# Graph attention on one core: gathers with a row limit, so that edges outside a visit's block are not fetched

## The chip, the cores and the metric

The kernel runs on one core of a Trainium2 chip. The metric is the device time of one execution in microseconds (us); the time before is the median of three runs. Nothing else runs on the core.

## The reference, cut to what matters

Three graph attention layers over 3125 nodes and 50000 edges, then a mixture-of-experts step. Only the attention layer matters here; the edges are sorted by their target `dst`.

```python
z = (x @ W).reshape(N, num_heads, head_dim)          # 12 x 64, 12 x 64, 1 x 768
el = jnp.sum(z * attn_l, axis=-1)
er = jnp.sum(z * attn_r, axis=-1)
e = jax.nn.leaky_relu(el[src] + er[dst], NEG_SLOPE)
m = jax.ops.segment_max(e, dst, num_segments=N)
ex = jnp.exp(e - m[dst])
denom = jax.ops.segment_sum(ex, dst, num_segments=N)
msg = (ex / denom[dst])[:, :, None] * z[src]
out = jax.ops.segment_sum(msg, dst, num_segments=N) + z + bias
```

## The kernel before

Nodes stand in 25 blocks of 128 (`NB`, padded to `NPAD` = 3200 rows). Each of the three layers has two parts. The node sweep multiplies every block by the weights and writes rows of `z` with the heads' `el` behind them to a table in device memory (`table[l]`, 792 floats used per row in layers 0 and 1, 769 in layer 2). The edge sweep then goes over the edges.

Edges stand in 391 tiles of 128 (50048 places, 48 of them padding). A tile whose edges belong to two blocks of targets is visited twice, once for each block: 391 + 24 = 415 visits (`V`), in 83 groups of 5 (`G`). The table `src_k` holds for each visit the 128 source rows, `dst_k` the target's place inside the visit's block. A place outside 0 to 127 gives a one-hot column of zeros in `S`, so such an edge adds nothing to the sum.

For each visit GpSimd issues one indirect DMA (L672) that gathers 128 table rows into one of 20 row buffers (`U` = 20: 15 in `arena`, 5 in `W`). It waits until the visit 20 places earlier has been summed (`s_agg`). Completion is counted on that buffer's own semaphore `s_z`. VectorE waits for all five gathers of a group (L1475 in layers 0 and 1, L1457 in layer 2), forms the exponents from them (L1475 and L1480), ScalarE takes the exponential, VectorE multiplies each row by its weight (L1492; the result stands in the row buffer itself), and TensorE adds the visit up with the one-hot `S` (L1047), which frees the buffer. Where a visit's place among the 20 is in `SPLIT`, ScalarE and VectorE split the row in two parts (L781, L1509; L785, L1512 and L1513 in layer 2), so that TensorE can take the faster number format. VectorE also makes the transposed one-hot from byte codes once a group (L1445). In layer 2 the one head's weight goes into the one-hot (`S_weighted`, L1498), and VectorE has less to do.

GpSimd's queue is written out for all 1245 gathers; each one is queued behind the one before it. VectorE's order within a group is fixed by `weigh`: message 0, message 1, then the steps of the next group's exponents between messages 1 to 3.

`tables` (L1279 to L1286 of the kernel before) makes `src_k` and `dst_k` once, before the first node sweep. TensorE's first node sweep and GpSimd's first gathers wait for it (`s_tables`).

Of the kernel before, what the change touches and what calls it, by code (L numbers as in the profile page):

```python
# [8 lines left out]
I32 = mybir.dt.int32  # L9
U32 = mybir.dt.uint32  # L10
U8 = mybir.dt.uint8
ALU = mybir.AluOpType
# [3 lines left out]
P = 128  # L16
# [3 lines left out]
NPAD = NB * P  # L20
# [8 lines left out]
ER_LEAD = 3  # L29
U = G * NBUF  # L30
VISITS = ET + NB - 1
V = -(-VISITS // G) * G
NG = V // G
# [14 lines left out]
NS = (TOP * N + EX * (P - 1)) // P  # L48
# [8 lines left out]
class Chain:  # L57
# [5 lines left out]
    def link(self, instruction):  # L63

        self.mark(instruction)
        self.follow()
# [33 lines left out]
def gnn_ffn(nc, x, edges, gnn, ffn, out):  # L100
    with ExitStack() as ctx:
        def sb(name, shape, dt=F32):
            return ctx.enter_context(nc.sbuf_tensor(name, shape, dt))

        def sem(name):
            return ctx.enter_context(nc.semaphore(name))
# [9 lines left out]
        PS = ctx.enter_context(nc.psum_tensor("PS", [P, 8, 512], F32))  # L116
# [19 lines left out]
        with nc.sbuf_tensor("xT_rest", [P, 2, D], F32R) as xT_rest:  # L136
            with nc.sbuf_tensor("local_rows", [P, 4 * P], BF16) as local_rows:
                below = EX * 2 * 2 * HALF - KC * (D + 2 * HMAX) - 2 * D - 2 * P
# [27 lines left out]
        src_k = sb("src_k", [P, V], I32)  # L166
        dst_k = sb("dst_k", [P, V])
        b_k = sb("b_k", [1, V + 1], I32)
        b_g = sb("b_g", [1, NG, 4], I32)
        b_of = sb("b_of", [1, NG + ER_LEAD, 8], I32)  # L170
        ends = sb("ends", [1, NB], I32)
        turns = sb("turns", [1, NS], I32)
        erm = sb("erm", [P, NB, 2 * HMAX])
        ert = sb("ert", [P, NB, HMAX])
        erp = sb("erp", [P, NB * 3 * 2 * HMAX], BF16)
# [19 lines left out]
        wu = sb("wu", [P, G, 2 * HMAX])  # L195
# [9 lines left out]
        def rows_buf(j, q, width=D):  # L205
            return arena[:, (2 * j + q) * D:(2 * j + q) * D + width]
# [4 lines left out]
        in0, in1, in2, xr, xT, x2 = (lambda q, j=j: rows_buf(j, q) for j in range(6))  # L211
# [22 lines left out]
        s_z = [sem(f"s_z{j}") for j in range(U)]  # L234
# [22 lines left out]
        def sweep_nodes(eng, stages, chain=None, per=0, count=NB, rolled=True, start=0):  # L257


            def steps(i, ts):  # L260
                for t in ts:
                    for stage, lead in stages:
                        if i is not None or 0 <= t + lead < count:
                            stage(Block(t + lead, i))

            if not rolled:
                steps(None, range(-max(lead for _, lead in stages), count - min(lead for _, lead in stages)))
                return
            steps(None, range(start - max(lead for _, lead in stages), 2))
            trips = (count - 4) // 2  # L270
            with eng.Fori(1, 1 + trips) as i:
                if chain:
                    chain.enter(i - 1, per)
                steps(i, (0, 1))
            if chain:
                chain.leave(trips)
            steps(None, range(2 + 2 * trips, count - min(lead for _, lead in stages)))
# [24 lines left out]
        def table_width(l):  # L302
            return D + (2 * HEADS[l] if HEADS[l] > 1 else 1)

        def slot_width(l):

            return D + 2 * HEADS[l]
# [10 lines left out]
        def edge_row(l, at):  # L318
            return group_rows(l, at // G)[:, at % G, :]

        def edge_heads(l, jj, n=1):
            return group_rows(l, jj)[:, :, D:D + n * HEADS[l]]
# [4 lines left out]
        def er_of(l, jj):  # L327
            return group_bank(jj)[:, 0:G * 2 * HEADS[l]].rearrange("p (g h) -> p g h", g=G)
# [11 lines left out]
        def uses(jj):  # L340

            return NI if jj < LAST_GROUPS else NI - 1

        def prep(at, n):
            return ST[:, :, :, :].rearrange("p a b c -> p (a b c)")[:, at:at + n]
# [4 lines left out]
        def bk_f():  # L350
            return prep(V, V)
# [4 lines left out]
        def rows_f():  # L356
            return prep(3 * V, 4 * 2 * P)
# [224 lines left out]
        def _(pool):  # L582
# [70 lines left out]
            for l in range(3):  # L653
                if l == 1:
                    pool.wait_ge(s_base, 16 * NB)
                    pool.wait_ge(s_spare, 16)
                    pool.wait_ge(s_last_bias, 16)
                if l == 2:
                    pool.wait_ge(s_bias_added, 16 * NB)
                sweep_nodes(pool, [(store(l), 0)])  # L660
                pool.wait_ge(s_stored[0], 16 * (NB // 2 + 1) * (l + 1))
                pool.wait_ge(s_stored[1], 16 * (NB // 2) * (l + 1))
                pool.wait_ge(s_tab, NB * (l + 1))
                pool.wait_ge(s_tables, 1)
                pool.wait_ge(s_filled, 16 * 2 * 3)
                pool.sem_inc(s_tick)
                for k in range(V):
                    pool.wait_ge(s_agg, V * l + k + 1)
                    if l == 2 and k == 12 * D // slot_width(l):
                        for q in range(2):  # L670
                            pool.wait_ge(s_x_kept[q], 16 * (NB // 2 + 1 - q))
                    nc.gpsimd.indirect_dma_start(  # L672
                        edge_row(l, k % U)[:, 0:table_width(l)], None, table[l][:, :],
                        bass.IndirectOffsetOnAxis(src_k[:, k:k + 1].bitcast(U32), 0)).then_inc(s_z[k % U], 16)

            for b in range(NB):
                keep_rows(b)
# [521 lines left out]
        def _(dve):  # L1199
            dc = Chain(dve, s_dve)  # L1200
            link = dc.link
# [10 lines left out]
            def augment_first(ks):  # L1212
                for k in ks:
                    for j in range(2):
# [14 lines left out]
            below = rows_f()[:, 0:(NB - 1) * 4].rearrange("p (b c) -> p b c", c=4)  # L1229
# [9 lines left out]
                                                op0=ALU.add, op1=ALU.add))  # L1239
            link(nc.vector.scalar_tensor_tensor(out=enter_at, in0=own[0:NB - 1, :], scalar=1.0, in1=PS[0:NB - 1, 1, 4:5],  # L1240
                                                op0=ALU.add, op1=ALU.add))
# [10 lines left out]
                                                op0=ALU.mult, op1=ALU.add))  # L1252
# [25 lines left out]

            def tables():  # L1279
                dve.wait_ge(s_turned, 1)  # L1280
                link(nc.vector.tensor_copy(src_k[:, :], PS[:, 2, 0:V]))
                link(nc.vector.scalar_tensor_tensor(out=dst_k[:, :], in0=bk_f(), scalar=-float(P), in1=PS[:, 3, 0:V],
                                                    op0=ALU.mult, op1=ALU.add))
                if V > VISITS:
                    link(nc.vector.memset(dst_k[:, VISITS:V], NO_NODE))
                dve.sem_inc(s_tables, 1)  # L1286

            W_parts = [(l, k, j) for l in (1, 2) for k in range(KC) for j in range(2)]
# [150 lines left out]
            def edge_sweep(l):  # L1439
                H = HEADS[l]  # L1440
# [7 lines left out]
                def exponents(g, i, jj):  # L1448

                    er = er_of(l, jj)  # L1450
                    t, u = wt[:, jj, :, 0:H], wu[:, :, 0:H]

                    def logits():
                        dve.wait_ge(s_er, g + (NG * l + 1))
                        for j in range(jj * G, (jj + 1) * G):
                            dve.wait_ge(s_z[j], 16 * i + 16 * (uses(jj) * l + 1))
                        dc.mark(nc.vector.tensor_tensor(u, edge_heads(l, jj), er[:, :, 0:H], ALU.add))  # L1457

                    def leaky():
                        dc.follow()  # L1460
                        dc.mark(nc.vector.scalar_tensor_tensor(out=u, in0=u, scalar=SLOPE, in1=u, op0=ALU.mult, op1=ALU.max))

                    def less_bound():
                        dc.follow()
                        dc.mark(nc.vector.tensor_tensor(u, u, er[:, :, H:2 * H], ALU.subtract))

                    def limit():
                        dc.follow()
                        nc.vector.tensor_scalar(t, u, 0.0, None, ALU.min).then_inc(s_pre, 1)

                    def both_logits():
                        dve.wait_ge(s_er, g + (NG * l + 1))
                        for j in range(jj * G, (jj + 1) * G):
                            dve.wait_ge(s_z[j], 16 * i + 16 * (uses(jj) * l + 1))
                        dc.mark(nc.vector.scalar_tensor_tensor(out=wu[:, :, 0:2 * H], in0=edge_heads(l, jj, 2), scalar=shift[:, 0:1],  # L1475
                                                               in1=er, op0=ALU.subtract, op1=ALU.add))

                    def higher():
                        dc.follow()
                        nc.vector.tensor_tensor(t, u, wu[:, :, H:2 * H], ALU.max).then_inc(s_pre, 1)  # L1480

                    if H > 1:
                        return both_logits, higher
                    return logits, leaky, less_bound, limit
# [235 lines left out]
            t = routing("t")[:, 0:EX * EX].rearrange("p (e f) -> p e f", f=EX)  # L1720
# [3 lines left out]
            t = routing("t").rearrange("p (m e) -> p m e", e=EX)  # L1724
# [135 lines left out]
```

## Time and profile before

| | us |
|---|---|
| runs | 2811.25, 2812.51, 2815.1 (median 2812.51) |
| span of the profiled execution | 3059.8 |

The profile has no other time of its own for that execution; its span runs from the first to the last instruction and is the time that the rows below are read against. It is 247.3 us longer than the median of the runs. Set-up and the first node sweep end at about 246 us, the three edge sweeps lie at about 246 to 906, 1095 to 1760 and 1960 to 2610 us, with a node sweep ahead of each, and the experts' part fills the last 300 us.

### The profile page before, as it was taken

To read this page: it belongs to the slowest core of one execution; us is meant where nothing else is said; L and a number is where in the kernel's file an instruction comes from. 1 tells how busy PE (TensorE), PEld (TensorE's weight loads), DVE (VectorE), ACT (ScalarE), POOL (GpSimd) and SP (SyncE) were. 2 spreads that over 40 slices of the span, in tenths; PEclk is the share of its full clock that TensorE was granted. 3 is DMA by queue.
4 is the path that set the end of the run, shared out by engine and by line. 5 is a ranking of instruction groups with operands and counts; after the bars stand their busy time and mean duration, and the time that the engine had idled before them with its cause. 6 is when DMAs were issued, how large, how long until landed. Compare 5 with 4: busy or idle time off the path is not lost.

```text
span 3059.8 us, 57119 instructions
## 1 busy us (share of the span) xinstructions
PE 2691.3 (88%) x14056; PEld 1838.6 (60%) x14060; DVE 2096.8 (69%) x3895; ACT 1244.9 (41%) x2607; POOL 1506.0 (49%) x1528
## 2 busy tenths in 40 slices
PE   3997999998989979898989999788898889759998
PEld 2884555555558855555555578555555555547776
DVE  6776888888887768888878877545555555673332
ACT  1224555555544435555555544223222223622211
POOL 1005666666631156666666412466666665114443
PEclk9998999999999979999999999899999999979999
DMA  6447888888867878888888767788888887967776
GB/s 210 169 148 251 289 286 291 291 290 290 289 219 205 210 228 292 289 287 290 291 287 288 250 191 216 218 281 285 279 282 281 282 282 258 397 217 145 145 146 118
DMA packets 199261, 762.09 MB, mean 249 GB/s; under 512 B 41889, under 2 KB 58033, under 8 KB 198542
## 3 DMA queue, kind: packets, MB, share of 16 engines
q0 software_dynamic: 127632, 604.14, 64.8%
q1 hardware_dynamic: 53790, 108.21, 11.6%
q10 hardware_dynamic: 17760, 48.79, 4.0%
q8 instruction: 36, 0.59, 0.1%
q14 instruction: 43, 0.35, 0.0%
HBM read 640.01 MB, written 133.45 MB: 253 GB/s over the span
## 4 chain that ended last, share of the span: by engine, by line
PE 50%; DVE 21%; issue 13%; ACT 4%; DMA 4%; another core or an unknown queue 3%; SPq 2%; POOL 1%; DVEq 1%; ACTq 1%; POOLq 0%
PE PS L1047 30%; DVE arena L1492 5%; PE PS L1176 5%; PE PS L978 4%; PE PS L1165 4%; PE PS L980 2%; DVE parts L1509 2%; PE PS L1022 2%; DMA arena<-table,src_k 2%; SPq L493 1%; DVE ST_b L1445 1%; DVE arena L1357 1%; DVE arena L1367 1%; DVE arena L1335 1%
## 5 line engine op out<-in xcount | busy, mean ns | idle before, releaser
L672 POOL DMA_INDIRECT arena<-table,src_k x945 | 959.9, 1016 | 500.8 <-issue 213.1
L1047 PE MATMUL PS<-arena,S 128*128 128x384 f32 (+1 forms) x1848 | 706.8, 514 | 57.8 <-issue 46.3
L1492 DVE TENSOR_TENSOR arena<-arena,PS 128x768 f32<-128x768 f32 x630 | 575.2, 946 | 0.9 <-ACT arena L822 0.9
L1047 PEld LDWEIGHTS PS<-arena,S 128*128 128x128 f32 x1848 | 335.5, 194 | 282.7 <-issue 156.8
L1047 PE MATMUL PS<-parts,S 128*128 128x384 f32 (+2 forms) x1332 | 340.4, 375 | 57.2 <-issue 51.0
L672 POOL DMA_INDIRECT W<-table,src_k x300 | 295.9, 986 | 160.5 <-PE PS L1047 71.2
L1047 PE MATMUL PS<-arena,S_weighted 128*128 128x384 f32 (+1 forms) x840 | 319.9, 516 | 33.4 <-issue 25.3
L1022 PEld LDWEIGHTS PS<-erp,ST_b 128*128 128x128 bf16 x3735 | 193.9, 97 | 249.9 <-issue 184.2
L618 POOL DMA_DIRECT2D table<-arena x75 | 41.6, 555 | 557.7 <-DVEq L1379 382.3
L1047 PEld LDWEIGHTS PS<-parts,S 128*128 128x128 f32 x1332 | 223.7, 192 | 106.0 <-issue 97.5
L830 ACT ACTIVATE apart<-iota_row,dst_k 128x128 f32<-128x128 f32 x830 | 261.7, 389 | 60.8 <-issue 44.1
L781 ACT ACTIVATE parts<-arena 128x780 fp32r<-128x780 f32 x168 | 142.0, 849 | 309.2 <-DVE arena L1492 136.7
L1022 PE MATMUL PS<-erp,ST_b 128*128 x3735 | 213.0, 172 | 54.0 <-issue 38.9
L1047 PE MATMUL PS<-W,S 128*128 128x396 f32 (+1 forms) x640 | 239.8, 502 | 14.6 <-issue 8.1
L1047 PEld LDWEIGHTS PS<-arena,S_weighted 128*128 128x128 f32 x840 | 154.3, 196 | 143.7 <-issue 79.4
L978 PE MATMUL PS<-W_lead,S 128*128 128x512 f32 x450 | 190.4, 423 | 9.8 <-DVE xT_rest L1383 7.9
L1509 DVE TENSOR_TENSOR parts<-arena,parts 128x780 fp32r<-128x780 f32 x168 | 162.0, 964 | 35.7 <-issue 24.4
L1492 DVE TENSOR_TENSOR W<-W,PS 128x768 f32<-128x768 f32 x200 | 182.4, 944 | 0.0
L978 PE MATMUL PS<-W_lead,xT_rest 128*128 128x512 f32 x450 | 179.2, 398 | 0.0
L978 PE MATMUL PS<-W_rest_r,S 128*128 128x512 f32 x450 | 178.7, 397 | 0.0
L1047 PEld LDWEIGHTS PS<-W,S 128*128 128x128 f32 x640 | 116.1, 190 | 91.3 <-issue 39.0
L1795 DVE TENSOR_SCALAR arena<-PS,gate_of 128x768 f32<-128x768 f32 x56 | 57.0, 1018 | 162.5 <-PE PS L1176 162.5
(293 smaller groups left out, 4354.1 us busy)
## 6 DMA issues: line engine op xcount, KB each, us to landing
arena<-mixed SPq DMA_DIRECT2D x63, 384.0 KB, 3.6
table<-arena POOLq DMA_DIRECT2D x50, 396.0 KB, 3.3
local_b<-local SPq DMA_DIRECT2D x123, 160.0 KB
mixed<-sums ACTq DMA_DIRECT2D x50, 384.0 KB
arena<-table SPq DMA_DIRECT2D x50, 384.0 KB, 4.6
arena<-table,src_k POOLq DMA_INDIRECT x945
table<-arena POOLq DMA_DIRECT2D x25, 384.5 KB, 4.6
out<-last_bias POOLq DMA_DIRECT2D x25, 384.0 KB, 6.4
```

The costliest lines, as they stand in the source:

```text
L672: nc.gpsimd.indirect_dma_start(edge_row(l, k % U)[:, 0:table_width(l)], None, table[l][:, :], bass.IndirectOffsetOnAxis(src_k[:, k:k + 1]. ...
L781: nc.scalar.activation(parts[:, n, 0, 0:D + H], row[:, 0:D + H], ACT.Copy).then_inc(s_leading, 1)
L830: o = nc.scalar.activation(apart[:, j, :], iota_row[:, :], ACT.Abs, scale=-1.0, bias=dst_k[:, bass.ds(g * G + j, 1)])
L978: nc.tensor.matmul(PS[:, 4 + 2 * b.q, :], rows[x_part], W_parts[W_part][:, 0:512], start=start, stop=stop)
L980: o = nc.tensor.matmul(PS[:, 5 + 2 * b.q, 0:z_width(l) - 512], rows[x_part], W_parts[W_part][:, 512:z_width(l)], start=start, stop=stop)
L1022: o = nc.tensor.matmul(er_of(l, jj)[:, j, :], ST_b[:, jj, j * P:(j + 1) * P], erp[:, bass.ds(b * (6 * H) + part * 2 * H, 2 * H)], start=(p ...
L1047: o = nc.tensor.matmul(flat[:, bass.ds(odd * 1024 + 512 * c, n)], onehot, row[:, c * HALF:c * HALF + n], start=False, stop=True, skip_grou ...
L1165: o = nc.tensor.matmul(to, token_xT(b.q)[:, k * P:(k + 1) * P], WiT[:, k, bass.ds(e * FF, FF)], start=(k == 0), stop=(k == KC - 1))
L1176: o = nc.tensor.matmul(PS[:, 4 + 2 * b.q + c, 0:HALF], hT(b.q)[0:rows, j * P:(j + 1) * P], flat[0:rows, bass.ds(e * (2 * D) + (2 * c + j) ...
L1492: nc.vector.tensor_tensor(z, z, a, ALU.mult).then_inc(s_msg, 1)
L1509: nc.vector.tensor_tensor(low[:, 0:D + H], row[:, 0:D + H], f32(high[:, 0:D + H]), ALU.subtract).then_inc(s_rest, 1)
L1795: nc.vector.tensor_scalar(zr(b.q, D).rearrange("p (c d) -> p c d", c=2), PS[:, 4 + 2 * b.q:6 + 2 * b.q, 0:HALF], gate_of[:, bass.ds(b.n, 1 ...
```

## The change

It passes a limit to the indirect DMA (`bounds_check`), under which a row whose source index lies past `NPAD` - 1 is not fetched and raises no error. `tables` adds `NPAD` or more to the source of every edge whose place lies outside the visit's block, for visits from the 21st on (`U:`). The first 20 visits fetch all rows, so that every row buffer holds finite numbers. What a skipped row's buffer holds afterwards is that of an earlier visit, so the exponents of layers 0 and 1 are held at or below zero (`higher`). Three small tables become bytes instead of 32-bit integers (`b_g`, `b_of`, `turns`). The limit is handed over in a register of GpSimd's queue, which is written again ahead of each gather; the wait for `s_agg` then stands on that register instruction instead of the gather.

```diff
@@ -166,10 +166,10 @@
-        b_g = sb("b_g", [1, NG, 4], I32)
-        b_of = sb("b_of", [1, NG + ER_LEAD, 8], I32)
+        b_g = sb("b_g", [1, NG, 4], U8)
+        b_of = sb("b_of", [1, NG + ER_LEAD, 8], U8)
         ends = sb("ends", [1, NB], I32)
-        turns = sb("turns", [1, NS], I32)
+        turns = sb("turns", [1, NS], U8)
@@ -671,7 +671,8 @@
                     nc.gpsimd.indirect_dma_start(
                         edge_row(l, k % U)[:, 0:table_width(l)], None, table[l][:, :],
-                        bass.IndirectOffsetOnAxis(src_k[:, k:k + 1].bitcast(U32), 0)).then_inc(s_z[k % U], 16)
+                        bass.IndirectOffsetOnAxis(src_k[:, k:k + 1].bitcast(U32), 0),
+                        bounds_check=NPAD - 1, oob_is_err=False).then_inc(s_z[k % U], 16)
@@ -1278,11 +1279,16 @@
                 dve.wait_ge(s_turned, 1)
-                link(nc.vector.tensor_copy(src_k[:, :], PS[:, 2, 0:V]))
                 link(nc.vector.scalar_tensor_tensor(out=dst_k[:, :], in0=bk_f(), scalar=-float(P), in1=PS[:, 3, 0:V],
                                                     op0=ALU.mult, op1=ALU.add))
                 if V > VISITS:
                     link(nc.vector.memset(dst_k[:, VISITS:V], NO_NODE))
+                link(nc.vector.tensor_copy(src_k[:, 0:U], PS[:, 2, 0:U]))
+                below, beyond = prep(2 * V, V - U), prep(3 * V, V - U)
+                link(nc.vector.tensor_scalar(below, dst_k[:, U:], 0.0, float(NPAD), ALU.is_lt, ALU.mult))
+                link(nc.vector.tensor_scalar(beyond, dst_k[:, U:], float(P), float(NPAD), ALU.is_ge, ALU.mult))
+                link(nc.vector.tensor_tensor(below, below, beyond, ALU.add))
+                link(nc.vector.tensor_tensor(src_k[:, U:], below, PS[:, 2, U:V], ALU.add))
                 dve.sem_inc(s_tables, 1)
@@ -1477,7 +1483,8 @@
                     def higher():
                         dc.follow()
-                        nc.vector.tensor_tensor(t, u, wu[:, :, H:2 * H], ALU.max).then_inc(s_pre, 1)
+                        nc.vector.scalar_tensor_tensor(out=t, in0=u, scalar=0.0, in1=wu[:, :, H:2 * H],
+                                                       op0=ALU.min, op1=ALU.max).then_inc(s_pre, 1)
```

On VectorE, at the end of the set-up before the first node sweep, the kernel before has these rows (the table of sources first, then that of places):

```order
L1342 TENSOR_TENSOR W_rest_r<-W,W_lead 128x792 x6
L1281 CAST src_k<-PS 128x415
L1282 SCALAR_TENSOR_TENSOR dst_k<-ST,PS 128x415
L1402 MEMSET gm 128x12
L1310 BN_STATS stats<-arena 128x6
```

The changed kernel has at the same place:

```order
L1348 TENSOR_TENSOR W_rest_r<-W,W_lead 128x792 x6
L1282 SCALAR_TENSOR_TENSOR dst_k<-ST,PS 128x415
L1286 CAST src_k<-PS 128x20
L1288 TENSOR_SCALAR ST<-dst_k 128x395
L1289 TENSOR_SCALAR ST<-dst_k 128x395
L1290 TENSOR_TENSOR ST<-ST 128x395
L1291 TENSOR_TENSOR src_k<-ST,PS 128x395
L1408 MEMSET gm 128x12
L1316 BN_STATS stats<-arena 128x6
```

Four instructions are added, each over 395 columns, and one shrinks from 415 columns to 20; nothing else of VectorE's order moves there.

On VectorE, within a group of an edge sweep of layers 0 and 1, the kernel before has:

```order
L1445 TENSOR_SCALAR ST_b<-local_b,own_code 128x640
L1475 SCALAR_TENSOR_TENSOR wu<-arena,shift,PS 128x120
L1492 TENSOR_TENSOR arena<-arena,PS 128x768
L1480 TENSOR_TENSOR wt<-wu 128x60
L1492 TENSOR_TENSOR arena<-arena,PS 128x768 x2
```

The changed kernel has:

```order
L1451 TENSOR_SCALAR ST_b<-local_b,own_code 128x640
L1481 SCALAR_TENSOR_TENSOR wu<-arena,shift,PS 128x120
L1499 TENSOR_TENSOR arena<-arena,PS 128x768
L1486 SCALAR_TENSOR_TENSOR wt<-wu 128x60
L1499 TENSOR_TENSOR arena<-arena,PS 128x768 x2
```

No row moves: one instruction of a group changes its kind. TensorE's, ScalarE's and SyncE's rows are the same in both kernels.

## Rows read from the trace of the kernel before

**Rows 1.** Busy time in stretches: 57 to 237 node sweep, 400 to 800 edge sweep, and so on.
```profile
core 0: us, PE busy (x) PEld busy (x) DVE busy (x) ACT busy (x) POOL busy (x), PEclk, DMA share, GB/s
57.00:237.00 180.00, 178.04 (x1030) 157.79 (x1031) 127.37 (x265) 44.70 (x73) 13.10 (x24) 1.00 0.47 162
400.00:800.00 400.00, 361.66 (x1801) 215.85 (x1800) 331.39 (x479) 221.00 (x526) 264.00 (x261) 0.98 0.88 289
906.00:1087.00 181.00, 176.10 (x989) 151.42 (x989) 136.56 (x214) 78.96 (x96) 31.50 (x44) 0.98 0.76 199
1200.00:1600.00 400.00, 359.82 (x1823) 215.20 (x1823) 334.48 (x482) 218.16 (x519) 263.90 (x260) 0.99 0.88 289
2100.00:2500.00 400.00, 356.80 (x1825) 216.90 (x1824) 216.16 (x677) 114.00 (x251) 255.87 (x261) 0.99 0.87 282
2747.00:3044.00 297.00, 296.29 (x1537) 232.40 (x1534) 93.41 (x166) 57.68 (x109) 136.18 (x105) 1.00 0.72 139
```

**Rows 2.** What VectorE waited for, 400 to 800 us: us in total, times, longest.
```profile
DVE wu L1475 <- remote: 43.4, 28, 4.2
DVE parts L1509 <- ACT parts L781: 9.2, 3, 4.7
DVE wu L1475 <- DMA W<-table,src_k: 6.0, 3, 2.3
DVE wu L1475 <- DMA arena<-table,src_k: 5.1, 4, 1.7
```

**Rows 3.** The same, 2100 to 2500 us (layer 2).
```profile
DVE wu L1457 <- remote: 103.3, 40, 6.5
DVE parts L1512 <- ACT parts L785: 45.0, 9, 7.7
```

**Rows 4.** GpSimd's gathers by line, whole execution: durations min/median/max, and what ended its idle time.
```profile
L672 POOL DMA_INDIRECT arena<-table,src_k x945: 941/950/1745, 246.3 to 2588.6; - x189
L672 POOL DMA_INDIRECT W<-table,src_k x300: 941/950/1727, 267.7 to 2566.0; - x150
  issue: 279.7, 906
  PE PS L1047: 277.3, 265
```

**Rows 5.** GpSimd in order of time, layer 1: start, us, what, idle before.
```profile
1300.76 1.04 POOL L672 DMA_INDIRECT arena<-table,src_k  x1 [1.15 <-PE PS L1047]
1302.11 0.94 POOL L672 DMA_INDIRECT arena<-table,src_k  x1 [0.30 <-issue]
1303.35 0.95 POOL L672 DMA_INDIRECT arena<-table,src_k  x1 [0.30 <-issue]
...
1308.45 0.94 POOL L672 DMA_INDIRECT arena<-table,src_k  x1 [1.30 <-PE PS L1047]
```

**Rows 6.** GpSimd's groups by line, 400 to 800 us: count, busy, mean ns, idle before.
```profile
L672 POOL DMA_INDIRECT arena<-table,src_k x196 | 201.8, 1030 | 101.7 <-PE PS L1047 46.4 <-issue 42.0 <-remote 13.3
L672 POOL DMA_INDIRECT W<-table,src_k x65 | 64.6, 994 | 34.6 <-issue 15.5 <-PE PS L1047 14.5 <-remote 4.6
```

**Rows 7.** The same, 2100 to 2500 us (layer 2).
```profile
L672 POOL DMA_INDIRECT arena<-table,src_k x195 | 191.7, 983 | 109.2 <-issue 42.4 <-PE PS L1047 41.4 <-remote 25.4
```

**Rows 8.** The page's GpSimd group of plain table stores, 128 rows each.
```profile
L618 POOL DMA_DIRECT2D table<-arena x75 | 41.6, 555 | 557.7 <-DVEq L1379 382.3
```

**Rows 9.** VectorE's exponent instructions by line: durations min/median/max.
```profile
L1480 DVE TENSOR_TENSOR wt<-wu x166: 205/214/272, 259.2 to 1746.0; 128x60 f32<-128x60 f32 x166
L1475 DVE SCALAR_TENSOR_TENSOR wu<-arena,shift,PS x126: 319/338/341, 258.9 to 1744.9; 128x120 f32<-128x120 f32 x126
L1461 DVE SCALAR_TENSOR_TENSOR wu<-wu x83: 154/161/200, 1965.8 to 2595.0; 128x5 f32<-128x5 f32 x83
L1457 DVE TENSOR_TENSOR wu<-arena,PS x63: 144/165/168, 1965.6 to 2593.6; 128x5 f32<-128x5 f32 x63
```

**Rows 10.** VectorE in order of time around `tables`.
```profile
51.16 0.58 DVE L1281 CAST src_k<-PS 128x415 int32<-128x415 f32 x1
51.78 0.59 DVE L1282 SCALAR_TENSOR_TENSOR dst_k<-ST,PS 128x415 f32<-128x415 f32 x1
52.55 0.07 DVE L1402 MEMSET gm<- 128x12 f32 x1 [0.18 <-DVE dst_k L1282]
54.24 0.56 DVE L1310 BATCH_NORM_STATS2 stats<-arena 128x6 f32<-128x384 f32 x1 [1.63 <-DMA arena<-in_x]
```

**Rows 11.** The page's DMA queues: packets, MB, share of 16 engines.
```profile
q0 software_dynamic: 127632, 604.14, 64.8%
```

## Prediction

> **What bounds the kernel now.** I read the busy time by stretch first, to see which parts can move at all. In the node sweeps and in the experts' part TensorE is busy 99%, 97% and nearly 100% of the time at a granted clock of 0.98 or more [rows 1]. The change touches nothing there. The edge sweeps are different. They take 400 us for 261, 260 and 261 gathers [rows 1], that is 1.533, 1.538 and 1.533 us a visit, although layer 2 gives VectorE only 216 us of work in 400 where layers 0 and 1 give it 331 and 334. A pace that does not depend on VectorE's load points to something common: the gathers. The DMA engines are busy 0.87 to 0.88 of the time at 282 to 289 GB/s.
>
> Next I read what VectorE waits for. In layer 0 it waits for gathers at L1475 (the rows that end in "remote" and "DMA") 43.4 + 6.0 + 5.1 = 54.5 us in 400, or 0.209 us a visit [rows 2]. Little else holds it, so its own pace without that wait would be 1.533 - 0.209 = 1.324 us. In layer 2 it waits 103.3 us for gathers [rows 3], but VectorE has slack there.
>
> Last comes GpSimd. Of 1245 gathers, 906 had only the fixed gap of about 0.30 us ahead of them [rows 4]; the timeline shows bursts of them, then one wait of more than 1 us for TensorE to free a buffer [rows 5]. Its own pace in layer 0 is (201.8 + 64.6)/261 + 0.30 = 1.321 us [rows 6], in layer 2 about 0.983 + 0.30 = 1.283 us [rows 7]. So VectorE and GpSimd are within 0.01 us of each other in layers 0 and 1, and both wait in the profiled execution on landings.
>
> **The profiled execution and the timed one.** The span is 3059.8 us, the median 2812.51. TensorE's stretches at 97% and more leave hardly any of the 247.3 us, so I put it on the 1245 visits: 0.199 us each. The timed visit then takes about 1.538 - 0.199 = 1.339 us. That is a choice, and the most important one here: it says that in a timed run most of the waiting for gathers (0.209 us a visit in layer 0) is already absent.
>
> **The change, part by part.**
>
> *Rows left out.* 415 visits ask for 53120 rows; 50000 are edges of their block, so 3120 are not. A block has about 2000 edges, 16 visits, so the first 20 visits contain one boundary, whose 128 rows are still fetched: 2992 rows a sweep are skipped, 5.6%, in all 8976. If every visit were set by the gathers' transfer, the profiled execution would gain 0.056 x 1.538 = 0.087 us a visit, 108 us over 1245. At the timed pace that is 0.056 x 1.339 = 0.075 us, 94 us, but the visit can't become shorter than the next bound. In layers 0 and 1 that is VectorE's 1.324: (1.339 - 1.324) x 830 = 12 us. In layer 2 it is GpSimd's 1.283: 0.056 x 415 = 23 us. Together 35 us at most. The other end is 0: if the landings no longer end any wait in the timed run. I take 25, since five gathers must land together and a queue seldom empties fully.
>
> *The register and the check on GpSimd.* No row shows a gather with a limit, nor a register write ahead of one. Below, the extra cost is 0: the check may be in the loop already, and the register write may lie under the gather before it. Less than nothing is possible for the two gathers at each boundary, which have half the descriptors to write; 72 boundaries by half of 0.95 us twice would be 68 us of GpSimd's time, most of which is not on the path. Above, the nearest rows are the indirect gather at 950 ns [rows 4] against the plain store of 128 rows at 555 ns [rows 8]: looking up 128 addresses costs at most 395 ns, 3.1 ns a row. A compare for each row should not cost more than half of that, 0.2 us. As GpSimd's pace in layers 0 and 1 (1.321) is only 0.018 below the timed visit, nearly all of an extra cost enters. For my forecast I take 0 to 0.02 us, so nothing; the larger values are a rival below. Behind a gather that waits stand all later gathers, and behind these VectorE's L1475.
>
> *tables.* Four instructions over 395 columns; the rows with 415 columns took 0.58 and 0.59 us [rows 10], so 4 x 0.57 = 2.3 us, less about 0.45 for the cast that shrinks to 20 columns: 1.8 us. Behind them VectorE sat idle 1.63 us for the first block of `x`, so 0.2 us shows. If that load came earlier, it would be 1.8. I take 0.2.
>
> *higher.* The old instruction takes 214 ns for 60 columns [rows 9]. The same two kinds over 5 columns take 161 and 165 ns, so the kind costs nothing: 0 us. The bound is the 338 ns of the same kind over 120 columns: 0.124 x 166 = 21 us; nearest is the 5-column pair, so I take 1 us.
>
> *Byte tables.* They are smaller and are read by as many instructions. 0 us.
>
> Sum against the span: 3059.8 - 108 + 1 is about 2955 if transfers bind there throughout; I expect about two thirds, near 2990. Sum against the median: 2812.5 - 25 + 0.2 + 1 = 2788.7, so 2789 us.
>
> **A rule beside it.** In this trace the gathers' landings end VectorE's waits at 289 GB/s [rows 1, 2]. The Trainium skill (DMA: Bandwidth & Descriptors, Anatomy of one DMA) gives a DMA of this kind about 2.0 us plus its bytes by 436 GB/s. By that a gather of 405.5 KB moves in 0.93 us, an estimate from that page, well inside every visit, and leaving rows out would gain nothing; the sum would be 2813.7. The rows of the profiled execution disagree, those of a timed run can't say.
>
> **Rivals.**
>
> *A: transfers still bind a little, GpSimd's extra is small.* 2789 us, range 2766 to 2806 (below: half of the 94 us, if the timed run waits for gathers more than the 1.339 us says; above: a quarter of the 25). For it: half of the groups wait for gathers in the profile. Chance 0.42.
>
> *B: the transfer is hidden anyway.* The whole 0.209 us is an effect of the profiled execution; VectorE and GpSimd at 1.32 set the timed pace. Then a shorter queue changes nothing: 2812.5 + 1.2, so 2808 to 2818. For it: 1.339 is that close to 1.324. Against it: layer 2, where VectorE is idle 46% of the time and the pace is no better. This holds too the case that a skipped row takes as long in the queue as a fetched one. Chance 0.18.
>
> *C: the check makes GpSimd the bound.* Place: the emission of L672. With x us more for each gather its pace is 1.321 + x in layers 0 and 1 and 1.283 + x in layer 2. It decides from 0.018 in the former and 0.056 in the latter. At x = 0.1: 0.082 x 830 + 0.044 x 415 = 86 us, 2898 us. At 0.05: 27 us, 2839 us. At 0.2: 211 us, 3023 us. For it: one instruction more for each gather, the wait moved off the gather, a compare for each of 128 rows, and no slack. Against it: all that the lookup costs is 3.1 ns a row, and the register write can lie under the gather before it. In the profiled execution, whose visit takes 1.538, this would not show as a loss up to 0.2 us. Chance 0.40.
>
> **How the numbers follow.** The likeliest is A, by little: 2789. The range leaves out the upper part of C, 0.13 (above x = 0.1), and 0.05 below 2766: 2766 to 2900. A difference under 0.2% (5.6 us) can't be told from no change. Faster 0.42, same 0.18, slower 0.40.
>
> **What would show it.** Right: fewer packets in the software queue by about 4500 of 127632 [rows 11] and 28 MB less; a shorter wait at VectorE's L1475 (now at another line); a profiled span well below 3059.8; GpSimd's gathers still at 0.95 us with a gap of 0.30. C shows as a longer gather or gap and a larger share of gathers with nothing but the gap ahead. B shows as a shorter span with unchanged runs and unchanged gathers. The weakest step is the 1.339 us: if the timed run waits for gathers more than I think, the gain is up to 94 us.

## The result and the profile after

The changed kernel is slower: 3023.69 us against 2811.88 us, a ratio of 1.0744 (95% interval 1.0722 to 1.0765). That is 212 us more. 2789 us was forecast, and the time lies outside the range of 2766 to 2900. One of its four runs (3743.59 us, at a mean granted clock of 0.654 where the others had 0.973 to 0.976) is a slow one and left out of the ratio. The profiled execution has a span of 3018.0 us and took 3019.67 us itself, so here the span and the runs agree.

Busy time in the same stretches of the edge sweeps, layers 0, 1 and 2 (columns as in [rows 1]):

```profile
400.00:800.00 400.00, 361.17 (x1850) 208.21 (x1851) 337.08 (x491) 224.07 (x537) 276.29 (x263) 1.00 0.86 278
1200.00:1600.00 400.00, 359.14 (x1837) 206.56 (x1836) 330.14 (x481) 218.93 (x524) 274.02 (x262) 1.00 0.85 276
2100.00:2500.00 400.00, 360.42 (x1862) 210.95 (x1861) 222.23 (x699) 118.34 (x261) 290.71 (x267) 1.00 0.85 274
```

The pace is 1.521, 1.527 and 1.498 us a visit. Beside [rows 1] this looks like a small gain (1.533, 1.538, 1.533). The runs say the opposite, because the profiled execution of before was 247 us slower than its own runs. No wait read from that trace may be compared with this one as it stands; further down stands what that trace has in common with a batch in which the kernel before took 3066 us.

What VectorE waited for, 400 to 800 us, and then 2100 to 2500 us:

```profile
DVE parts L1516 <- ACT parts L782: 24.1, 12, 5.0
DVE wu L1481 <- DMA arena<-table,src_k: 17.7, 15, 2.9
DVE wu L1481 <- PE PS L1023: 17.0, 17, 2.6
DVE wu L1481 <- DMA W<-table,src_k: 7.0, 4, 2.5
...
DVE wu L1463 <- DMA arena<-table,src_k: 46.1, 14, 5.3
DVE wu L1463 <- PE PS L1023: 44.7, 21, 3.2
```

L1481 is the old L1475, L1463 the old L1457, L1023 the old L1022. Against [rows 2] and [rows 3] the rows that end in "remote" are gone and a new releaser has come: `PE PS L1023`, the products of `er` with the one-hot (`er_of_edges`), which in these stretches of the trace of before released none. TensorE is late. But it is busy only 361 us in 400, so it is held up by something that isn't a matmul.

The page's queue row and its row of gathers, then two rows of TensorE's queue (`PEldq` in the profile), `blocks_of` (L1013) and the register operations of `add_up` (L1040), with durations min/median/max:

```profile
q0 software_dynamic: 127632, 576.01, 63.2%
L672 POOL DMA_INDIRECT arena<-table,src_k x945 | 1014.4, 1073 | 408.8 <-issue 226.3
L1013 PEldq TENSOR_LOAD <-b_of x498: 1216/1222/2532, 252.0 to 2552.9; - x166
L1040 PEldq ALU_OP  x640: 32/32/32, 266.4 to 2544.5; - x160
```

Three things are to be seen. The bytes fell by 28.1 MB from [rows 11], as forecast, but the packets did not: 127632 in both, so no packet falls away. 4458 more packets than before are under 512 bytes (46347 against 41889 in the pages), about one for two of the 8976 rows. A gather is longer: mean 1073 ns. And TensorE's queue spends 1222 ns, 498 times (twice a group), on reading five block numbers into registers from the table `b_of`. Not one row of the prediction was about this load. In the kernel before, with words in place of bytes, the same two rows of TensorE's queue read:

```profile
L1012 PEldq TENSOR_LOAD <-b_of x498: 5/582/1751, 249.9 to 2596.9; - x166
L1039 PEldq ALU_OP  x640: 2/32/755, 262.3 to 2588.9; - x160
```

The added instructions of `tables` in the changed kernel, in order of time (start, us, what, idle before):

```profile
51.11 0.18 DVE L1286 CAST src_k<-PS 128x20 int32<-128x20 f32 x1
51.32 0.37 DVE L1288 TENSOR_SCALAR ST<-dst_k 128x395 f32<-128x395 f32 x1
51.72 0.36 DVE L1289 TENSOR_SCALAR ST<-dst_k 128x395 f32<-128x395 f32 x1
52.12 0.57 DVE L1290 TENSOR_TENSOR ST<-ST 128x395 f32<-128x395 f32 x1
52.73 0.57 DVE L1291 TENSOR_TENSOR src_k<-ST,PS 128x395 int32<-128x395 f32 x1
53.48 0.07 DVE L1408 MEMSET gm<- 128x12 f32 x1 [0.18 <-DVE src_k L1291]
55.39 0.56 DVE L1316 BATCH_NORM_STATS2 stats<-arena 128x6 f32<-128x384 f32 x1 [1.85 <-DMA arena<-in_x]
...
L1486 DVE SCALAR_TENSOR_TENSOR wt<-wu x166: 204/213/278, 262.8 to 1723.1; 128x60 f32<-128x60 f32 x166
```

The last row is the new `higher`: 213 ns against 214 [rows 9]. Behind the added four VectorE still sits idle 1.85 us for the first block of `x`, so most of them is hidden. The first BATCH_NORM_STATS2 starts at 55.60 us in x2 and at 55.19 in x1 (two kernels of the second batch below, with and without the added four), so about 0.4 us shows. `higher` costs nothing.

### The profile page after: what moved, and what is told of

Same layout as the page of the kernel before. It is cut to its first block, busy times and chain, and to the rows that moved or that the text cites. A ratio compares the mean times of both kernels' runs of the same rounds, so it can differ in the third digit from the quotient of the medians.

```text
span 3018.0 us, 58368 instructions
## 1 busy us (share of the span) xinstructions
PE 2665.2 (88%) x14056; PEld 1784.5 (59%) x14060; DVE 2084.3 (69%) x3899; ACT 1241.7 (41%) x2607; POOL 1584.4 (52%) x1528
## 2 busy tenths in 40 slices
DMA packets 199271, 734.04 MB, mean 243 GB/s; under 512 B 46347, under 2 KB 62491, under 8 KB 198542
## 3 DMA queue, kind: packets, MB, share of 16 engines
q0 software_dynamic: 127632, 576.01, 63.2%
## 4 chain that ended last, share of the span: by engine, by line
PE 53%; DVE 15%; issue 12%; DMA 9%; ACT 4%; POOL 3%; SPq 2%; ACTq 1%; DVEq 1%; POOLq 0%
PE PS L1048 32%; DMA arena<-table,src_k 6%; PE PS L1177 5%; PE PS L979 4%; PE PS L1166 4%; PE PS L981 2%; DVE arena L1499 2%; POOL arena L672 2%; PE PS L1023 2%; DMA W<-table,src_k 2%; SPq L493 2%; DVE W L1499 1%; DVE arena L1341 1%; DVE arena L1363 1%; DVE arena L1362 1%
## 5 line engine op out<-in xcount | busy, mean ns | idle before, releaser
L672 POOL DMA_INDIRECT arena<-table,src_k x945 | 1014.4, 1073 | 408.8 <-issue 226.3
L1048 PEld LDWEIGHTS PS<-arena,S 128*128 128x128 f32 x1848 | 326.4, 191 | 338.5 <-issue 212.8
L672 POOL DMA_INDIRECT W<-table,src_k x300 | 318.6, 1062 | 121.8 <-issue 74.4
L1048 PE MATMUL PS<-parts,S 128*128 128x384 f32 (+2 forms) x1332 | 323.9, 365 | 25.4 <-issue 12.0
L1048 PE MATMUL PS<-arena,S_weighted 128*128 128x384 f32 (+1 forms) x840 | 313.8, 504 | 34.1 <-issue 20.1
L1023 PEld LDWEIGHTS PS<-erp,ST_b 128*128 128x128 bf16 x3735 | 173.8, 96 | 200.0 <-issue 135.2
L1048 PE MATMUL PS<-W,S 128*128 128x396 f32 (+1 forms) x640 | 247.0, 508 | 20.8 <-DVE arena L1499 13.1
L1048 PEld LDWEIGHTS PS<-arena,S_weighted 128*128 128x128 f32 x840 | 148.0, 190 | 148.9 <-issue 81.1
L1023 PE MATMUL PS<-erp,ST_b 128*128 x3735 | 182.1, 171 | 23.8 <-DVE ST_b L1451 16.2
L650 POOL DMA_INDIRECT out<-arena,target_of x56 | 89.1, 1591 | 159.1 <-DMA out<-arena,target_of 128.8
```

Of the source, the lines that this page charges most:

```text
L650: nc.gpsimd.indirect_dma_start(out[:, :], bass.IndirectOffsetOnAxis(target_of[:, n:n + 1].bitcast(U32), 0), zr(n % 2, D), None, compute_op ...
L672: nc.gpsimd.indirect_dma_start(edge_row(l, k % U)[:, 0:table_width(l)], None, table[l][:, :], bass.IndirectOffsetOnAxis(src_k[:, k:k + 1]. ...
L1023: o = nc.tensor.matmul(er_of(l, jj)[:, j, :], ST_b[:, jj, j * P:(j + 1) * P], erp[:, bass.ds(b * (6 * H) + part * 2 * H, 2 * H)], start=(p ...
L1048: o = nc.tensor.matmul(flat[:, bass.ds(odd * 1024 + 512 * c, n)], onehot, row[:, c * HALF:c * HALF + n], start=False, stop=True, skip_grou ...
```

## The experiments

Two theories went in: one of the parts that GpSimd executes (limit, register, wait apart) costs some 0.17 us a visit; or the byte tables cost it, on TensorE's queue. The kernels of one batch were run together with the kernel before; ratios are to it, and its median there is given.

### First: one part of the change at a time (before: 2811.93 us)

**e1, the byte tables alone.**

```diff
-        b_g = sb("b_g", [1, NG, 4], I32)
-        b_of = sb("b_of", [1, NG + ER_LEAD, 8], I32)
+        b_g = sb("b_g", [1, NG, 4], U8)
+        b_of = sb("b_of", [1, NG + ER_LEAD, 8], U8)
...
-        turns = sb("turns", [1, NS], I32)
+        turns = sb("turns", [1, NS], U8)
```

> The kernel before with the three small tables as bytes, and nothing else of the change. Theory W (the wait that moved from the gather to the register write ahead of it takes the slack away) and theory L (the limit itself makes each gather longer) both say no change: ratio 1.00. Theory B (byte tables make the register loads of TensorE or ScalarE slower) says up to the whole 212 us, ratio 1.07.

**e2, the byte tables and the limit**, no row left out (the lines of e1 and this one):

```diff
+                        bounds_check=NPAD - 1, oob_is_err=False).then_inc(s_z[k % U], 16)
```

> The kernel before with byte tables and the limit on every gather, but with the table of sources as before, so that no row lies past the limit and none is left out. Theories W and L say that the loss is all here or more of it, since no row is saved: ratio 1.07 to 1.09. Theory S (rows that are left out cost GpSimd or the queue more than rows that are fetched) says ratio 1.00.

**e3, the whole change, with the limit in a register that is written once**:

```diff
+            limit_reg = nc.alloc_register(mybir.EngineType.Pool, "row_limit")
+            nc.gpsimd.reg_mov(limit_reg, NPAD - 1)
+            limit = nc.gpsimd.snap(limit_reg)
...
-                        bounds_check=NPAD - 1, oob_is_err=False)
+                        bounds_check=limit, oob_is_err=False)
```

> The changed kernel, but the limit is put in a register once, ahead of all gathers, so each gather carries its own wait again and no register write stands before it. Theory W says the loss is gone and the skipped rows may gain a little: ratio 0.99 to 1.00, span near 2800 us. Theories L and S say it stays: ratio 1.07.

**e4, e1 with an instruction ahead of each gather that carries the wait**:

```diff
+                    pool.sem_inc(s_tick)
                     nc.gpsimd.indirect_dma_start(
```

> The kernel before with byte tables and no limit, but ahead of each gather stands a small instruction of GpSimd's queue that carries the wait (it adds 1 to a semaphore that nobody waits for). Theory W says ratio 1.07 as in the changed kernel. Theories L, S and B say 1.00.

Measured: e1 3022.57 us (1.0752 [1.0734, 1.077]), e2 3024.86 (1.0757 [1.0739, 1.0775]), e3 3019.21 (1.0737 [1.0719, 1.0755]), e4 3021.75 (1.0747 [1.0729, 1.0765]). The byte tables alone are the whole loss, and nothing that is added to them or taken from the rest moves it. In e1 TensorE's load takes 1222 ns again, and VectorE waits for TensorE (2100 to 2500 us):

```profile
L1012 PEldq TENSOR_LOAD <-b_of x498: 1216/1222/2597, 251.7 to 2554.7; - x166
...
DVE wu L1457 <- PE PS L1022: 80.1, 35, 3.0
```

The theory of the bytes stands, that of GpSimd's parts as the cause of the 212 us falls. That e2 equals e1 doesn't make the limit free: behind a pace of about 1.5 us a visit an extra of 0.1 us on GpSimd need not show. This had to be tried again without the bytes.

### Second: which table, and the change without it (before: 2809.5 us)

**x1, e1 with `b_of` as words again.** `b_g` and `turns` stay bytes; the loaded numbers are also held at or above zero, so that the kernel differs from before by that too.

```diff
-        b_of = sb("b_of", [1, NG + ER_LEAD, 8], U8)
+        b_of = sb("b_of", [1, NG + ER_LEAD, 8], I32)
...
-                    return nc.values_load_multi_w_load_instructions(
+                    return [smax(b, 0) for b in nc.values_load_multi_w_load_instructions(
```

> The kernel of e1 (byte tables), but TensorE's table of block numbers (b_of) is words again, and each number that is read from it is held at zero or above before use, which costs a few register operations. Theory R (TensorE's register load of five block numbers takes 1222 ns from bytes and 582 ns from words, 498 times, 319 us in all, and two thirds of that show) says that the loss is gone: ratio 1.00 to 1.02, the rest being the added register operations. Theory P (the smaller tables move every later tensor in on-chip memory, and that is what costs) says 1.03 or more, since two of the three tables stay small. Theory G (ScalarE's table b_g as bytes costs) says 1.07.

**x5, e1 with each byte table padded to the size it had as words**, so that each group's numbers lie as far apart as in the kernel before (`b_of` shown; `b_g` and `turns` likewise):

```diff
-        b_of = sb("b_of", [1, NG + ER_LEAD, 8], U8)
+        b_of = sb("b_of", [1, NG + ER_LEAD, 32], U8)
```

> The kernel of e1 with byte tables that are padded to the size of the word tables, so that every other tensor lies where it lay before. Theory R says ratio 1.075, as e1. Theory P says 1.00.

**x2, the whole change with `b_of` as in x1.**

> The changed kernel in full, with TensorE's block numbers as words, held at zero or above. If only the byte loads made the change slow, this is x1 plus the limit and the rows left out, at a visit of about 1.34 us. My case A (transfers still bind a little) says 10 to 35 us below x1, case B (hidden) the same as x1 within 5 us, case C (the check makes GpSimd the bound) above x1: with the 0.055 us that the trace of the changed kernel shows on each gather, 1.321 + 0.055 = 1.376 us against 1.34, up to 30 us above.

**x3, x1 and the limit**, no row left out.

> x1 with the limit on every gather and no row past it. Case C says 20 to 40 us above x1, since the check costs and nothing is saved; cases A and B say within 5 us of x1. Against x2 it gives what the 8976 rows are worth.

Measured: x1 2808.53 us (0.9996 [0.9982, 1.0009]), x5 3024.88 (1.077 [1.0743, 1.0797]), x2 2904.81 (1.0339 [1.0313, 1.0365]), x3 2901.82 (1.0332 [1.031, 1.0354]). So the loss is in `b_of` alone, not in where it lies and not in the other two tables. The two block numbers that ScalarE loads from `b_g` are bytes in x1 too, and take 473 ns there against 494 from words in the trace of before, so there bytes are not the dearer kind. x3 against x1 prices the limit, with all rows fetched: 93 us. x2 against x3 prices the rows left out: 3 us more, within the intervals, so nothing.

x1 equals the kernel before in time, and its profile stands in for the one that the prediction lacked, at the timed pace (span 2811.0 us). TensorE's queue, its stretches in layers 0, 1 and 2, and the gathers:

```profile
L1013 PEldq TENSOR_LOAD <-b_of x498: 577/583/1805, 250.7 to 2345.5; - x166
L1040 PEldq ALU_OP  x640: 32/32/32, 263.3 to 2333.7; - x160
...
400.00:800.00 400.00, 383.30 (x2068) 239.50 (x2066) 375.41 (x547) 248.98 (x597) 310.71 (x294) 1.00 0.94 326
1200.00:1500.00 300.00, 295.40 (x1599) 185.63 (x1598) 294.95 (x424) 192.97 (x463) 229.28 (x231) 1.00 0.95 340
1900.00:2300.00 400.00, 386.16 (x2126) 248.41 (x2127) 253.08 (x792) 135.00 (x297) 307.58 (x304) 1.00 0.94 330
...
L673 POOL DMA_INDIRECT arena<-table,src_k x945: 940/948/1757, 247.1 to 2336.6; - x189
  issue: 292.2, 952
  PE PS L1048: 89.5, 291
```

The pace is 1.361, 1.299 and 1.316 us a visit. All 1243 idle times of GpSimd ahead of a gather come to 381.7 us, 0.307 each: also where TensorE released the buffer, the gather followed at the fixed gap. GpSimd issues without a pause, and TensorE and VectorE are at 94% to 98% beside it in layers 0 and 1; the DMA engines carry 326 to 340 GB/s. In the chain of waits a group of x1 has TensorE's work end to end, and the same place of the changed kernel has gaps of "issue" (time in which the engine waits for nothing that the profile shows) just before `add_up`. The chain in the changed kernel, and the two loads of that stretch (L1013, 600 to 607 us, the later one 2107 ns long):

```profile
600.38 0.21 PE PS L1023 x9
600.59 1.41 PE PS L1048 x4
602.00 0.41 issue
602.41 1.57 PE PS L1048 x4
603.98 1.21 issue
605.19 1.57 PE PS L1048 x4
...
L1013 PEldq TENSOR_LOAD <-b_of x2: 1262/1684/2107, 600.7 to 602.7; - x2
```

x1, with its loads (613 to 620 us):

```profile
613.36 0.14 PE PS L1023 x6
613.50 2.12 PE PS L1048 x8
615.62 0.21 PE PS L1023 x9
615.83 4.03 PE PS L1048 x12
619.86 0.14 PE PS L1023 x6
...
L1013 PEldq TENSOR_LOAD <-b_of x2: 580/581/582, 615.5 to 616.9; - x2
```

In the changed kernel the first load runs from 600.7 to 602.0 us and the second from 602.7 to 604.8, and the matmuls behind each start 0.4 us after its end. The second ends 0.8 us after the matmuls ahead of it. In x1 both loads lie under running matmuls.

The limit's price stands in the gathers of x3:

```profile
L673 POOLq MOVE  x1245: 29/29/29, 246.6 to 2415.1; - x178
L673 POOL DMA_INDIRECT arena<-table,src_k x945: 994/1002/1798, 247.4 to 2425.8; - x189
...
L673 POOL DMA_INDIRECT arena<-table,src_k x945 | 1043.8, 1105 | 294.5 <-issue 235.6 <-PE PS L1049 51.5 <-DMA table<-arena 7.4
```

The median rises from 948 to 1002 ns, the mean from 1027 (x1, the same group) to 1105. The register write ahead is 29 ns. Over all 1245 gathers GpSimd's busy time rises from 1276.9 us (x1) to 1367.2, so by 90 us or 0.073 each; 93 were measured.

### Third: the parts on the fast base, and what a gather costs

Four kernels. **y1**: x2 with e3's single register. **y2**: x1 with e4's wait apart. **s1**: x2, with the limit leaving out all rows of partitions 64 to 127 too, from visit 21 on, so that half of the edges are missing from the sums (rows with a place below 0 in partitions 0 to 63 are fetched again, which adds nothing to a sum):

```diff
-                link(nc.vector.tensor_scalar(below, dst_k[:, U:], 0.0, float(NPAD), ALU.is_lt, ALU.mult))
+                link(nc.vector.tensor_scalar(shift[:, :], own[:, 0:1], 64.0, float(NPAD), ALU.is_ge, ALU.mult))
+                link(nc.vector.tensor_scalar(below, dst_k[:, U:], 0.0, shift[:, 0:1], ALU.mult, ALU.add))
```

**s2**: x2 without the limit, where gathers from visit 21 on ask for partitions 0 to 63 alone; the other half keeps old rows.

```diff
+                    m = P if k < U else P // 2
-                        edge_row(l, k % U)[:, 0:table_width(l)], None, table[l][:, :],
-                        bass.IndirectOffsetOnAxis(src_k[:, k:k + 1].bitcast(U32), 0),
-                        bounds_check=NPAD - 1, oob_is_err=False).then_inc(s_z[k % U], 16)
+                        edge_row(l, k % U)[0:m, 0:table_width(l)], None, table[l][:, :],
+                        bass.IndirectOffsetOnAxis(src_k[0:m, k:k + 1].bitcast(U32), 0)).then_inc(s_z[k % U], 16)
```

> x2 (the changed kernel with TensorE's block numbers as words), but the limit is put in a register once, so that no register write stands ahead of a gather and each gather carries its own wait. Theory M (the register write, 29 ns on the queue in the trace of x2, and the wait on it cost the 95 us) says about 2810 us, ratio 1.00. Theory K (the check inside the gather costs: the trace of x1 has a median gather of 948 ns, that of x2 of 1002 ns) says about 2900 us, ratio 1.03, and gathers of 1002 ns.

> x1 (no limit), but a small instruction of GpSimd's queue with the wait on it stands ahead of each gather. Theory M says about 2900 us, theory K about 2810 us with gathers of 948 ns.

> x2, but beside the rows outside the block every row for partitions 64 to 127 is left out too, from the 21st visit on (so half of all edges are wrong). Theory K with skipped rows as dear as fetched ones (x2 and x3 differ by 3 us though 8976 rows are left out) says 2890 to 2910 us and gathers of about 1000 ns, with the DMA engines half idle. If a skipped row costs GpSimd nothing, the gather falls towards 0.55 us and the time to about 2760 us. If a skipped row costs it more than a fetched one, the time rises above 2910 us.

> x2 without the limit, and from the 21st visit of each sweep on every gather asks only for the rows of partitions 0 to 63 (half of the edges are wrong). If GpSimd's emission sets the pace of 1.31 us that the trace of x1 shows in all three sweeps (gathers back to back with a gap of 0.30 us), the pace falls to VectorE's 1.28 us in layers 0 and 1 and to TensorE's in layer 2: 2730 to 2780 us. If the transfers or the loop over 20 buffers set it, also less, but x2 against x3 speaks against transfers. If TensorE or VectorE set it already: 2800 us or more.

In this batch the kernel before itself takes 3065.91 us: y1 3068.38 (1.0007 [0.9998, 1.0017]), y2 3136.84 (1.0229 [1.0212, 1.0246]), s1 3121.64 (1.018 [1.016, 1.02]), s2 3067.17 (0.9997 [0.9987, 1.0008]). The answers don't fit the second batch, and 3066 us is the size of the span of 3059.8 us that the prediction works from. The expectations below speak of another chip. That isn't shown: the record has chip number 12 for this batch and for the first one, in which the kernel before took 2811.93 us. What differs between the batches is open. TensorE's queue shows in y1 what the trace of before showed, and the changed kernel (32/32/32) and x1 did not:

```profile
L1044 PEldq ALU_OP  x640: 2/32/1163, 264.6 to 2595.2; - x160
```

Register operations of 32 ns take up to 1.2 us there. And in s2, whose gathers bring half of the rows, VectorE's waits (400 to 800 us) still end in "remote", which stands for another core or an unknown queue:

```profile
DVE wu L1482 <- remote: 49.1, 30, 4.5
```

In y1, with all rows, the same wait comes to 49.0 us. So its length doesn't depend on the bytes. The four kernels were run again:

> The kernel of y1 once more, since on the chip of y1 to s2 the kernel before itself took 3066 us and TensorE's queue had stalls that hide the rest. Where the kernel before takes about 2810 us: theory M (the register write and the wait on it cost the 95 us) says about 2810 us; theory K (the check inside the gather costs, 1002 against 948 ns) about 2900 us.

> The kernel of y2 once more. Where the kernel before takes about 2810 us: theory M says about 2900 us, theory K about 2810 us.

> The kernel of s1 once more (half of the rows left out under the limit). Its trace on the other chip showed gathers of 1005 ns and the DMA engines busy 0.41 instead of 0.77 of the time. Where the kernel before takes about 2810 us: 2890 to 2910 us if GpSimd's gather sets the pace and transfers cost nothing; clearly under 2890 us if transfers still matter.

> The kernel of s2 once more (no limit, 64 rows a gather; gathers of 903 ns instead of 948). Where the kernel before takes about 2810 us: with GpSimd as the bound 45 ns by 1245 gathers, so up to 56 us less, 2755 to 2790 us; if another engine already sets the pace, 2800 us or more.

Measured, against a kernel before of 2807.25 us: r1 (= y1) 2904.19 (1.0331 [1.0298, 1.0363]), r2 (= y2) 2809.39 (1.0007 [0.9989, 1.0024]), r3 (= s1) 2896.03 (1.0302 [1.0274, 1.0329]), r4 (= s2) 2758.59 (0.9808 [0.9781, 0.9835]).

r1 equals x2 and r2 equals x1: neither writing the register nor the wait apart costs anything, so the 93 us are the check inside the gather. For r3 the gathers by line, then the stretch 400 to 800 us:

```profile
L673 POOL DMA_INDIRECT arena<-table,src_k x945: 994/1003/1799, 248.9 to 2422.4; - x189
...
400.00:800.00 400.00, 378.42 (x2013) 235.66 (x2013) 363.55 (x533) 243.28 (x579) 312.74 (x287) 0.99 0.53 170
```

With half of the rows left out the DMA engines fall from 0.90 (x2) to 0.53 of the time and from 297 to 170 GB/s, the gather stays at 1003 ns, and its ratio is 0.004 below that of x2, with overlapping intervals. At this pace transfers do not bind, and a row left out costs GpSimd what a fetched one does. The same rows of r4:

```profile
L674 POOL DMA_INDIRECT arena<-table,src_k x945: 892/905/1710, 246.3 to 2284.5; - x189
...
400.00:800.00 400.00, 398.18 (x2156) 255.62 (x2155) 396.41 (x575) 261.38 (x623) 288.30 (x297) 1.00 0.72 185
```

The gather is 43 ns shorter, 54 us over 1245, and 49 us are gained. r3 moves about as few bytes (361.87 MB in the software queue, r4 366.20) with a gather of 1003 ns and gains nothing, so the gain of r4 is most likely GpSimd's time. No run halves the bytes and keeps the gather at 948 ns, so the two aren't fully separated. TensorE and VectorE are then busy 398 and 396 us in 400: the next bound lies right behind.

No kernel here beats the one before and computes all of the reference; x1 and r2 equal it.

## Why the prediction was wrong, by its steps

**Byte tables: this step failed, and by itself it gives the whole 212 us (e1).** The prediction said that they are smaller, are read by as many instructions, and cost 0 us. It counted the instructions and didn't ask what one of them costs with the other element type, nor who is queued behind it. The load of five numbers takes 1222 ns from bytes and 583 ns from words. (1222 - 583) x 498 = 318 us of TensorE's queue; 212 us of it shows, 0.17 us a visit. The rows at 600 us say where: TensorE's matmuls stand behind the load in one queue, and the load comes twice a group in `body`, ahead of `add_up` and ahead of `er_of_edges`. The Trainium skill (DMA: Bandwidth & Descriptors, Latency and other measured facts) gives the floor of such a load as about 600 ns; the words' 582 and 583 ns agree with it, the bytes' 1222 are twice that, and ScalarE's two bytes at 473 are below it, so as a floor it doesn't hold here. Why five bytes take twice as long as five words, no run here shows. It is not the only step that failed: with the words back, x2 takes 2904.8 us, still slower and still outside the range.

**The check on GpSimd: the mechanism of rival C was right, its size was put too low in the forecast.** I took 0 to 0.02 us. It measured 0.054 us by the median gather and 0.073 by the mean of all, within the gather, and 93 us of time. The bound was sound (at most 0.2, against the plain store). Rival C's 2898 us at 0.1 is near x2's 2904.8 by luck: at 0.073 its own formula gives 53 us, since it grants the visit 0.018 and 0.056 us of slack, and x1 shows none. And the time on record is not rival C's: in the kernel as changed the check hides behind the byte loads (e2 against e1: 2 us), and the 3023 us that rival C has at 0.2 meets the result by coincidence. Its reasoning was that the lookup costs 3.1 ns a row, so halving rows would save much. r4 took 64 rows away and saved 43 ns, 0.7 ns a row; most of the 948 ns doesn't depend on the rows.

**Rows left out: 25 us forecast, 0 measured** (x2 against x3). Of the "what would show it" list the bytes came true (28.1 MB) and the packets didn't: none fell away. The step rested on the waits in [rows 2, 3] that end in "remote", read as waits for gathers' bytes. They did not follow the transfer: s2 has them with half the rows. In x1 VectorE's waits for landings are 18.5 us in 400, 0.063 us a visit instead of 0.209. Rival B's claim, that the transfer is hidden anyway, was right, and so is what the rule beside the sum says of them. By the Trainium skill (DMA: Bandwidth & Descriptors, Anatomy of one DMA) leaving rows out gains nothing, and r3 agrees. By the Trainium skill's figures there one gather would take about 2.9 us, an estimate from that page; the gathers of x1, issued every 1.3 us or so, take 5.7 us from issue to landing.

**The timed visit: 1.339 us was near, its reason was not.** x1 shows 1.361, 1.299 and 1.316. The 247 us between span and median were not waits that come with profiling. Span and median of the runs agree within 0.3% in every later trace, in the 3066 us batch too (3018.0 and 3023.69; 2811.0 and 2808.53; y1: 3067.6 and 3068.38), and the kernel before takes about 2810 us in three batches and 3066 in one. The profile of before is therefore most likely one of the condition of that batch; that its TensorE queue is what slows it is read from the rows alone (register operations up to 0.755 and 1.163 us, against 32 ns), not shown by an experiment. It would also explain why the changed profile's shorter span stands beside longer runs.

**Right:** GpSimd's pace in layers 0 and 1 and VectorE's are within a few hundredths of a microsecond (x1, r4); `tables` costs 0.4 us where 0.2 was forecast, and `higher` nothing.

## What to carry to other kernels

Where a table's element type changes, look at every instruction that reads it, register loads in an engine's queue above all, and at what is queued behind them. An edit that costs an engine nothing in one trace may be hidden by another edit of the same change: price the parts again with the costly one undone. When the profiled span stands several per cent off the runs, ask first whether both were taken in the same condition, and read no wait from it as a bound until a profile at the timed pace exists.

## What the hardware showed

- A load of five numbers into TensorE's registers: 582 to 583 ns from 32-bit words, 1222 ns from bytes, also when they lie as far apart as the words (x5: 1223). ScalarE's load of two numbers: 473 to 474 ns from bytes, 494 from words (the latter in the trace of before alone).
- An indirect gather of 128 rows takes GpSimd 948 ns, with a limit 1002, with a limit and half of the rows past it 1003, and one of 64 rows without a limit 905. Rows past the limit still make packets (127632 in all, in r3 too), only without their bytes; rows that are never asked for do not (r4: 89712).
- A register write ahead of each gather (29 ns), or an instruction that carries its wait, costs nothing, though GpSimd issues without a pause.
- The kernel before takes 2807 to 2812 us in three batches and 3066 in one, though two of these four, with 2811.93 and 3065.91 us, have the same chip number on record. In the latter single register operations of TensorE's queue take up to 1.4 us (y1), and an edit that costs 3.3% elsewhere costs 0.1% (y1, r1), while one that costs nothing elsewhere costs 2.3% (y2, r2). Why is open.
